# Two stacked LSTMs on one core: steps 0 to 2 without the scale of h, and x loaded in halves

## The reference, cut to what matters

```
x: 16 x 128 x 128 (batch, time, feature), h0 = cond: 16 x 128, all float32
def lstm(x, h0, Wx, Wh, b):            # c0 = 0, 128 steps in order
    h_bar = x[t] @ Wx + b + h @ Wh     # gates i, f, o, g: 4 x 128 columns
    c = sigmoid(f) * c + sigmoid(i) * tanh(g)
    h = sigmoid(o) * tanh(c)
x = x + linear_attention(lstm(x, cond, Wx1, Wh1, b1), W_theta, W_phi, W_g)
x = x + ffn(lstm(x, cond, Wx2, Wh2, b2), W1, fb1, W2, fb2)   # 128 -> 512 relu -> 128
```

## Time and profile before

| | us |
|---|---|
| median of 3 runs | 414.35 |
| lowest and highest run | 414.0, 414.84 |
| the profiled execution's own time | 414.66 |
| its span, first to last instruction | 412.7 |
| TensorE busy | 392.8 (95%) |
| VectorE busy | 273.1 (66%) |
| ScalarE busy | 206.7 (50%) |
| GpSimd busy | 8.1 (2%) |

### The profile page before, as it was taken

The page is one execution under the profiler, slowest core; times in us unless marked ns, Lnnn a source line. Parts: engine busy times, 40 slices in busy tenths (PEclk is TensorE's granted clock), DMA queues, the critical chain, the costliest instruction groups (busy, mean ns, idle before and its releaser), DMA issues.

```text
span 412.7 us, 14901 instructions
## 1 busy us (share of the span) xinstructions
PE 392.8 (95%) x4979; PEld 293.2 (71%) x4979; DVE 273.1 (66%) x1697; ACT 206.7 (50%) x1451; POOL 8.1 (2%) x20
## 2 busy tenths in 40 slices
PE   8999999999999999999999999999999999999996
PEld 6777666677666677666689877777777777777775
DVE  5676666665666666666668776666677666676664
ACT  3666555555544555544556444444444444444442
POOL 7000000000000000000000000000000000000000
PEclk9999999999999999999999999999999999999999
DMA  5111011111011111010000100000000000000000
GB/s 159 39 21 21 6 17 19 19 19 19 2 17 19 19 19 18 3 17 14 15 15 2 27 20 6 20 19 19 19 6 13 19 19 19 19 9 10 19 19 13
DMA packets 11697, 8.20 MB, mean 20 GB/s; under 512 B 1098, under 2 KB 11130, under 8 KB 11675
## 3 DMA queue, kind: packets, MB, share of 16 engines
q1 hardware_dynamic: 10842, 6.17, 7.5%
q0 software_dynamic: 544, 1.23, 1.0%
q10 hardware_dynamic: 288, 0.52, 0.4%
HBM read 2.87 MB, written 1.05 MB: 9 GB/s over the span
## 4 chain that ended last, share of the span: by engine, by line
PE 68%; DVE 17%; ACT 9%; issue 4%; DVEq 0%; ACTq 0%
PE fbank L413 22%; PE fbank L386 9%; DVE cell L1006 6%; DVE ring L1016 5%; ACT fgate L818 5%; DVE scan L1003 5%; ACT cell L836 5%; PE bankU L630 4%; PE bankV L407 4%; PE ibank L407 4%; PE gbank L407 3%; PE bankV L482 3%; PE bankY L637 2%; PE bankY L477 2%; PE bankU L515 2%
## 5 line engine op out<-in xcount | busy, mean ns | idle before, releaser
L413 PEld LDWEIGHTS fbank<-ring,whf 128*128 128x128 f32 x508 | 75.5, 188 | 77.9 <-DVE ring L1016 74.1
L386 PE MATMUL fbank<-warm_w 128*128 128x384 bf16 x537 | 125.2, 325 | 0.1
L818 ACT ACTIVATE fgate<-fbank 128x16 f32<-128x16 f32 x254 | 46.8, 184 | 139.3 <-PE fbank L413 138.9
L413 PE MATMUL fbank<-ring,whf 128*128 128x16 f32 x508 | 99.8, 272 | 15.1 <-DVE ring L1016 8.8
L1003 DVE TENSOR_TENSOR scan<-fgate,cell 128x16 f32<-128x16 f32 x254 | 43.7, 172 | 70.5 <-ACT fgate L818 61.1
L1016 DVE TENSOR_TENSOR ring<-cell,ogate_h 128x16 f32<-128x16 f32 x256 | 44.5, 174 | 41.7 <-ACT cell L836 41.3
L836 ACT ACTIVATE cell<-cell 128x16 f32<-128x16 f32 x256 | 43.0, 168 | 54.1 <-DVE cell L1006 53.9
L1006 DVE TENSOR_TENSOR_SCAN cell<-scan 128x32 f32<-128x32 f32 x256 | 59.4, 232 | 10.0 <-ACT scan L828 1.3
L407 PE MATMUL ibank<-h_hi,wh_parts 128*128 128x16 f16 x508 | 62.0, 169 | 0.0
L407 PEld LDWEIGHTS gbank<-h_hi,wh_parts 128*128 128x128 f16 x508 | 52.2, 137 | 0.0
L1021 DVE TENSOR_TENSOR h_lo<-ring,h_hi 128x16 f16<-128x16 f32 x256 | 44.9, 175 | 8.7
(11 more groups left out here) (189 smaller groups left out, 603.1 us busy)
## 6 DMA issues: line engine op xcount, KB each, us to landing
rows_t<-rows SPq DMA_DIRECT2D x16, 128.0 KB
x_rows<-in_x_dram SPq DMA_DIRECT2D x17, 64.0 KB
out_dram<-y_sb SPq DMA_DIRECT2D x16, 64.0 KB
xres<-x2T SPq DMA_DIRECT2D x15, 64.0 KB, 1.9
xin<-x2T SPq DMA_DIRECT2D x14, 64.0 KB, 1.8
w<-in_L_ffn_W_dram POOLq DMA_DIRECT2D x2, 256.0 KB, 4.0
wh<-in_L_cond_Wh_dram ACTq DMA_DIRECT2D x1, 256.0 KB, 3.0
wx<-in_L_cond_Wx_dram ACTq DMA_DIRECT2D x1, 256.0 KB, 3.5
```

The costliest lines, as they stand in the source:

```text
L386: nc.tensor.matmul(fbank[1 - p][:, P:4 * P], warm_w[:], warm_three, start=False, stop=True, skip_group_check=True)
L413: nc.tensor.matmul(step_out(p, t, GF), whf[layer][:], ring[:, (s - 1) % STEPS, :], start=False, stop=True, skip_group_check=True).then_inc ...
L818: nc.scalar.activation(fgate[:], fbank[p][:, NB * t:NB * t + NB], ACT.Sigmoid, scale=1.0 / Z_UNIT).then_inc(f_done[layer], 1)
```

## The change

Steps 0 and 1 of layer 1 give an h without the unit, kept in `h_first`; steps 1 and 2 multiply it, in float32, with the loaded float32 Wh in all four gates (`unscaled_step`). From step 2's h on, and from step 3's products on, all is as before. The high and low parts of Wh for i and o are made by GpSimd, from the two scaled copies; those of g still by ScalarE and VectorE. GpSimd also writes `h_first`, scaled, into `ring`. `top_product` comes behind the projections of g and i; the scales are filled beside steps 0 to 2. x's first chunk is loaded in two halves of 64 rows, by SyncE and by ScalarE; the condition comes by SyncE's queue. Before step 0 TensorE starts with the transposes, has one warm-up and two fillers less, and does the start products first and the projections last. The chunk 1 biases, projections and seeds move on by one or two steps. Semaphores of layer 2's weights are split.

```diff
@@ sync
-            sp.dma_start(x_rows[:, 0, :], x_ctb[0]).then_inc(rows_loaded[0], 16)
+            sp.dma_start(x_rows[0:P // 2, 0, :], x_ctb[0, 0:CH // 2]).then_inc(rows_loaded[0], 16)
+            sp.dma_start(cond_rows[:], cond).then_inc(cond_loaded, 16)
@@ gpsimd
-            pool.dma_start(cond_rows[:], cond).then_inc(cond_loaded, 16)
...
-            pool.dma_start(bias[1][0:1, :], l2_b.unsqueeze(0)).then_inc(weights2_loaded, 16)
-            pool.dma_start(wx[1][:], l2_wx).then_inc(weights2_loaded, 16)
+            pool.dma_start(bias[1][0:1, :], l2_b.unsqueeze(0)).then_inc(wx2_loaded, 16)
             pool.dma_start(wh[1][:], l2_wh).then_inc(wh2_loaded, 16)
+            pool.dma_start(wx[1][:], l2_wx).then_inc(wx2_loaded, 16)
+            pool.wait_ge(scale_made[0], 8)
+            nc.gpsimd.tensor_scalar(i_and_o(wh_parts[0][:, 0, :]), i_and_o(wh[0][:]), w_unit(0), None,
+                                    ALU.mult).then_inc(pool_parts, 1)
+            nc.gpsimd.tensor_scalar(i_and_o(wh_rest[:]), i_and_o(wh[0][:]), w_unit(0), None,
+                                    ALU.mult).then_inc(pool_parts, 1)
+            pool.wait_ge(pool_parts, 2)
+            nc.gpsimd.tensor_tensor(out=i_and_o(wh_parts[0][:, 1, :]), in0=i_and_o(wh_rest[:]),
+                                    in1=i_and_o(wh_parts[0][:, 0, :]), op=ALU.subtract).then_inc(pool_parts, 1)
+            pool.wait_ge(h_ready[0], 2)
+            nc.gpsimd.tensor_scalar(ring[:, 0:2, :], h_first[:], h_unit(0), 1.0 / Z_UNIT, ALU.mult,
+                                    ALU.mult).then_inc(first_kept, 1)
             pool.dma_start(w1[:], f_w1).then_inc(weights2_loaded, 16)
@@ tensor
+            def unscaled_step(s):
+
+                pe.wait_ge(h_ready[0], s)
+                for g, done in ((GF, f_ready), (GG, g_ready), (GI, i_ready), (GO, o_ready)):
+                    nc.tensor.matmul(step_out(0, s, g), wh[0][:, gate_cols(g)], h_first[:, s - 1, :], start=False,
+                                     stop=True, skip_group_check=True).then_inc(done[0], 1)
...
             pe.wait_ge(consts_ready, 1)
-            keep_warm(6)
+            keep_warm(5)
+            pe.wait_ge(half_loaded, 16)
+            pe.wait_ge(ident_ready, 2)
+            pe.wait_ge(rows_loaded[0], 16)
+            nc.tensor.transpose(bankU[:, 0:P], x_rows[:, 0, :], ident[:]).then_inc(x_transposed, 1)
+            pe.wait_ge(cond_loaded, 16)
+            nc.tensor.transpose(cell[:, P:P + NB], cond_rows[:], ident[0:NB, 0:NB]).then_inc(cond_transposed, 1)
             pe.wait_ge(consts_ready, 2)
             nc.tensor.matmul(bankV[:, :], zeros[:, 0:P], warm_four, start=True, stop=True, skip_group_check=True)
-            pe.wait_ge(ident_ready, 2)
-            fill(1, 2)
-            pe.wait_ge(rows_loaded[0], 16)
-            nc.tensor.transpose(bankU[:, 0:P], x_rows[:, 0, :], ident[:]).then_inc(x_transposed, 1)
-            top_product(0, fbank[1][:, 0:P])
             fill(1, 1)
-            pe.wait_ge(cond_loaded, 16)
-            nc.tensor.transpose(bankY[:, 0:NB], cond_rows[:], ident[0:NB, 0:NB]).then_inc(cond_transposed, 1)
+            pe.wait_ge(wh1_loaded, 16)
+            pe.wait_ge(h0_kept, 1)
+            initial(0, GG, start=True)
+            initial(0, GI, start=True)
             pe.wait_ge(bias1_loaded, 16)
-            bias_gate(0, 0, GG, start=True)
+            bias_gate(0, 0, GG)
+            bias_gate(0, 0, GI)
+            pe.wait_ge(wx1_loaded, 16)
             pe.wait_ge(xT_kept, 1)
-            pe.wait_ge(wx1_loaded, 16)
-            project_gate(0, 0, GG, xT[:, 0, :])
-            bias_gate(0, 0, GI, start=True)
-            project_gate(0, 0, GI, xT[:, 0, :])
-            pe.wait_ge(h0_kept, 1)
-            pe.wait_ge(wh1_loaded, 16)
-            initial(0, GG).then_inc(g_ready[0], 1)
-            initial(0, GI).then_inc(i_ready[0], 1)
+            project_gate(0, 0, GG, xT[:, 0, :]).then_inc(g_ready[0], 1)
+            project_gate(0, 0, GI, xT[:, 0, :]).then_inc(i_ready[0], 1)
+            top_product(0, bankY[:, 2 * P:3 * P])
...
+                if first and s == CH:
+                    pe.wait_ge(first_kept, 1)
...
-                if t == 0:
-                    if first and s == 0:
-                        pe.wait_ge(scale_made[0], 3)
+                if t == 0 and not no_history or first and s == 2:
                     bias_gate(int(last), 1 - p, GF)
...
-                if t == 2 and not last:
+                if not last and t == (3 if no_history else 2):
                     project_gate(0, 1 - p, GF, rhs(i, p))
...
-                    fill(0, (0, 0, 2, 2, 3, 0, 4, 3)[s])
+                    fill(0, (0, 0, 2, 2, 3, 0, 3, 4)[s])
...
-                    due = {3: (GG,), 4: (GI,), 5: (GO,)}
+                    due = {4: (GG,), 5: (GI,), 6: (GO,)}
...
-                if first and s in (0, 2, 3):
+                if first and s in (2, 3):
                     pe.wait_ge(o_done[0], s + 1)
-                    bias_gate(0, 1, SEEDED[max(s - 1, 0)]).then_inc(bias_spread, 1)
+                    for g in ((GG,), (GI, GO))[s - 2]:
+                        bias_gate(0, 1, g).then_inc(bias_spread, 1)
...
-                if s == 1:
-                    pe.wait_ge(parts_ready[0], 3)
...
+                if s == 3:
+                    pe.wait_ge(parts_ready[0], 2)
+                    pe.wait_ge(pool_parts, 3)
+                if s in (1, 2):
+                    unscaled_step(s)
@@ scalar
+            act.dma_start(x_rows[P // 2:P, 0, :], x_ctb[0, CH // 2:CH]).then_inc(half_loaded, 16)
             act.dma_start(wh[0][:], l1_wh).then_inc(wh1_loaded, 16)
...
-                if first:
-                    act.wait_ge(scale_made[0], SCALED - 2)
-                    high_of_first(GG)
-                    high_of_first(GI)
...
-                if first:
-                    high_of_first(GO)
...
-                if first and 2 <= s <= 4:
-                    keep_seeds(s - 2)
+                if first and 3 <= s <= 5:
+                    keep_seeds(s - 3)
...
+                if s == 1:
+                    act.wait_ge(scale_made[0], 8)
+                    nc.scalar.mul(part(0, 0, GG), wh[0][:, gate_cols(GG)], w_unit(0)).then_inc(high_ready, 1)
@@ vector
+            dve.sem_inc(hi_ready[0], 2)
+            dve.sem_inc(lo_ready[0], 2)
...
-            top_of(0, fbank[1][:, 0:P])
+            top_of(0, bankY[:, 2 * P:3 * P])
             power_of(0, 3)
             inverse_of(0, 5)
-            units_of(0, 6)
-            fills_of(0, 8)
-            nc.vector.tensor_scalar(whf[0][:], wh[0][:, gate_cols(GF)], w_unit(0), None,
-                                    ALU.mult).then_inc(parts_ready[0], 1)
-            rest_of_first(dve, GG)
-
+            def units_beside(s):
+
+                if s == 0:
+                    units_of(0, 6)
+                    dve.wait_ge(scale_made[0], 8)
+                    nc.vector.tensor_scalar(whf[0][:], wh[0][:, gate_cols(GF)], w_unit(0), None,
+                                            ALU.mult).then_inc(parts_ready[0], 1)
+                if s == 1:
+                    dve.wait_ge(high_ready, 1)
+                    nc.vector.scalar_tensor_tensor(out=part(0, 1, GG), in0=wh[0][:, gate_cols(GG)], scalar=w_unit(0),
+                                                   in1=part(0, 0, GG), op0=ALU.mult, op1=ALU.subtract
+                                                   ).then_inc(parts_ready[0], 1)
...
+                if unscaled and s == 1:
+                    fill_of(0, 8)
+                if unscaled and s == 2:
+                    pair_of(0)
...
-                nc.vector.tensor_tensor(out=ogate_h[:], in0=ogate[:], in1=unit_fill[layer][:],
+                nc.vector.tensor_tensor(out=ogate_h[:], in0=ogate[:],
+                                        in1=ones[:, 0:NB] if unscaled and s < 2 else unit_fill[layer][:],
                                         op=ALU.mult).then_inc(h_inputs[layer], 1)
                 dve.wait_ge(h_inputs[layer], n * 2 + 2)
+                if unscaled and s < 2:
+                    nc.vector.tensor_tensor(out=h_first[:, s, :], in0=tanhc, in1=ogate_h[:],
+                                            op=ALU.mult).then_inc(h_ready[layer], 1)
+                    return
...
+                dve.wait_ge(first_kept, 1)
                 nc.vector.tensor_copy(hist[:, p, :].rearrange("p (t b) -> p t b", b=NB),
```

More of the change, by code:

```diff
@@ L94, in build @@
         ogate_h = sb("ogate_h", [P, NB])
+        h_first = sb("h_first", [P, 2, NB])
         seeds = [sb(f"seeds{n}", [P, 3, P]) for n in (1, 2)]
@@ L192, in build @@
         bias_spread = sem("bias_spread")
+        pool_parts = sem("pool_parts")
+        first_kept = sem("first_kept")
+        half_loaded = sem("half_loaded")
+        wx2_loaded = sem("wx2_loaded")
         seeds2_kept = sem("seeds2_kept")
@@ L246, in part, with i_and_o @@
             return wh_parts[layer][:, which, gate_cols(g)]
[L248 to L255, removed]
+        def i_and_o(tile):
```

(56 more changed lines are left out.)

21 lines of the change are left out of this document (9 added, 12 removed).

## The result

| | before | after |
|---|---|---|
| median of the runs, us | 414.21 (6 runs, 414.0 to 414.84) | 419.01 (6 runs, 416.03 to 421.71) |
| the profiled execution, us | 414.66 | 418.18 |
| its span, us | 412.7 | 416.1 |

The ratio after to before is 1.0106, 95% interval 1.0069 to 1.0142: slower by 1.1%, and outside the forecast range. As striking as the median is the spread: 0.8 us became 5.7 us.

The account below looks back on a forecast made before the run. The prediction took regular steps to be bound by a loop of latencies and the opening by TensorE's order; its terms summed to +0.31 us, 414.97 for the profiled execution, 414.7 against the median, range 413.5 to 415.8.

Parts of the forecast that it names:

- term 1: Opening to h of step 0: new loads and TensorE order bring h at 8.64 instead of 8.98, -0.34 us.
- the clock rises late: Rival, opening: TensorE's level rises only after step 0, h at 9.65, one more microsecond, 415.7 us; chance 0.2.
- sign of error: Opening and later steps: forecast wrong if float32 pairs stay at 0.45 after 6.9, or steps behind 3 differ over 0.2.
- Terms 2 and 3: Steps 1 and 2: float32 pairs make step 1 longer by 0.16 us and step 2, behind attention weights, by 0.29.
- Term 4: Step 7: a fourth filler behind the spreading product ends later, +0.10 us (0 to 0.16).
- Term 5: Steps 1 and 2: GpSimd's operations and VectorE disturb each other, +0.10 us (bounds 0 and +0.6).
- The halves bring nothing: Rival, opening loads: x lands at 4.0, condition at 4.9, h of step 0 at 9.05, 415.1 us; chance 0.15.
- GpSimd holds VectorE: Rival, steps 1 and 2: whole GpSimd operations delay VectorE, or come late, 0.5 us more, 415.2; chance 0.15.
- Faster: Rival, opening: all loads land by 3.3, level rises before start products, h of step 0 at 7.7, 413.5 us; chance 0.12.

Follow-up runs that it names:

- b_thin: The kernel before without one warm-up product and the two fillers ahead of x's transpose; ratio 1.0021, eight of twelve executions at 413.9 to 414.42, four at 417.13 to 417.8.
- b_halves: The kernel before with only the new loads of x and the condition; ratio 1.0085, four of twelve executions at 415.06 to 415.19, eight at 418.51 to 420.78.
- a_fills2: The kernel after with one warm-up product and two opening fillers back, and five more fillers in steps 0 to 2; 415.27 us, ratio 1.0038.
- a_old_steps: The kernel after with the old loads, two more warm-ups and two more opening fillers, and five more fillers in steps 0 to 2; 414.93 us, ratio 1.0025.
- a_long: The kernel after with 20 more warm-up products ahead of everything; 420.39 us.
- b_long: The kernel before with 20 more warm-up products ahead of everything; 419.76 us.
- a_fills: The kernel after with the sixth warm-up product and two opening fillers back; 417.23 us, ratio 1.0077.
- a_pool_late: a_fills2 with GpSimd's three operations on Wh started only after h of step 1; 415.91 us, ratio 1.0039.
- a_whole: The kernel after with x in one transfer by SyncE again, the condition still second on SyncE's queue; 417.51 us, ratio 1.0089.

## Why the prediction was wrong

**The step that failed** is the clock inside term 1: "at its low level until about 6.6". The level was carried over from the old opening as if it were a point in time. The rival "the clock rises late" named the mechanism and its condition, the level still low when the gate projections start, and that is what happened (the first projection at 7.38, a pair at 0.43). It had a chance of 0.2, which was too low: the trace of before showed one execution only, while b_thin and b_halves show that small changes of the opening split the executions into groups 3 to 5.7 us apart. It was also priced too low. It had h of step 0 at 9.65, and the profiled execution has 10.41. The scan was nearly right (9.2 forecast, 9.49), but h was put 0.46 behind it, with the output gate done. That gate's bias, start product and projection come last and ran at the low level too, until 9.95, so h came 0.92 behind the scan. And the level's fall in steps 3 and 4, another 1.3, was in no case. The text's own sign of error, a float32 pair at 0.45 after 6.9, is what the chain shows; step 4, 0.97 longer than before, is another. That the change thins steps 1 and 2 (no float16 products, biases moved on) was worked out as time only, never as work that keeps the level up.

**Term 1**, -0.34. With the level high before the start products, h of step 0 is at 8.49 (a_fills2) and 8.47 (a_old_steps), near the 8.64 of the forecast, and the scan stands just behind VectorE's inverse (7.96 and 8.03 in a_fills2) as it said. But the base was an execution of before with a later rise: b_thin, the old order with the level high early, has it at 8.37. So the new order gains nothing at step 0 against an old one with an early level, and 0.13 when everything has landed (a_long against b_long). And the loads came other than assumed: "Wh and Wx are issued some 0.5 later" was 1.21. x at 3.7 was right (3.6 forecast). In the kernel after the late Wh is hidden, since TensorE at the low level gets to it only at 5.36; in a_fills2, with the level high, TensorE stands waiting for it until 5.38. Half a tile was assumed to cost part of the issue; the two halves took 0.75 and 1.16, the second ending 0.41 after the first. The Trainium skill (Perfetto Trace Analysis, DMA Instruction — HWDGE (DVE, Sync)) says that the time shown for an issue includes the wait for the lock of the descriptor generator, which two sequencers share. The trace agrees in two places: 1.16 is 0.41 over the other queue's 0.75, and in the kernel before SP's 0.80 is 0.40 over ACT's 0.40. Why the first half took 0.75 where all of Wh had taken 0.40 isn't told by that, and no run issued a half by itself.

**Terms 2 and 3**, +0.16 and +0.29. Right as a sum: h of step 2 was forecast at 1.78 + 2.10 = 3.88 after h of step 0 and came at 3.85 (a_fills). Step 1 without GpSimd is 1.79 (1.78 forecast). With GpSimd it is 2.01, and step 2 shrinks to 1.84, since the attention's products end it at the same time.

**Term 4**, +0.10: +0.06 (1.61 against 1.55 to h of step 8; every kernel with the new order has the fourth filler and this step, and none was run without it). **Term 5**, +0.10: GpSimd's operations took 1.01, 0.91 and 0.67, outside the 0.3 to 0.6 assumed for the first two, yet they ended at 13.56, before TensorE's step 3 needed them (first float16 product at 15.27). Their net cost is 0, the lower bound. The Trainium skill (SBUF — State Buffer, SBUF: two separate sides) has the shared port held for the whole instruction; the product lost 0.26 beside a GpSimd operation of 0.91, so the trace does not show a hold of that length.

**The other rivals.** *The halves bring nothing*: x did come 0.3 sooner than the 4.0 of that case, but what was queued behind its half came late, so the loads cost more than that case had. *GpSimd holds VectorE*: it does in step 1, for 0.26, and nothing of it is left at step 2. *Faster* needed all loads by 3.3; Wh landed at 5.3, and with the level up before the start products h of step 0 came at 8.49 and not at 7.7.

**Not in the sum:** step 3 +0.06, step 6 +0.16, and at step 160 -0.15 in the kernel after, -0.30 in most others with its order. Taken with the level high, terms 2 to 5 gave +0.65 and the steps to 8 show +0.70 (a_fills). That nearness is partly luck: term 5 measured 0, and 0.22 of the 0.70 are steps 3 and 6, which were in no term.

So, shown: the level's late rise and its fall are most of the loss (fillers alone give back 3.9 of 4.8 us), the loads cost 0.9 to 1.1 by themselves (in the old order), the order about 0.7 in steps 1 to 8. Argued only: that the long executions without a trace and with a mean clock of 0.999 or 1.0 rose late. Open: why the level rises at other times in executions of the same code, and why it falls at times in the old order too (b_long, b_halves).

## What to carry to other kernels

Work taken off TensorE in an opening, or in thin steps near it, can cost more than it saves: price a change there at both levels, and don't carry the moment of the rise over from the old order. A single profile doesn't tell how near a kernel is to the edge; the spread of its executions does, and leaving out one warm-up shows it. Before moving a load to another queue, see what is queued behind it there: the half tile of x arrived in time and made Wh 1.2 us late.

## What the runs showed of the hardware

- The level differs between executions of one kernel: a_fills2 and a_fills have the same code up to the end of the opening, and one profile has pairs at 0.22 from 5.77, the other only from after 9.5.
- The granted clock column reads 1.00 in the opening while the pairs take 0.43; only a fall after the first rise lowers it (0.76 and 0.81 in the kernel after, 0.61 in a_pool_late).
- The condition, 8 KB, needed 2.3 us from issue to landing second on SP's queue in the kernel after and 3.6 in a_whole: the size doesn't set it.
- VectorE has waits that no row explains: at step 160 before, 0.30 us after the gate it is said to wait for had ended, and at step 6 after, 0.38 us without a releaser.
